# GpSimd instead of VectorE for the attention's low token halves, in a four-layer convolution and attention kernel

## The reference

```python
# layer 0: three gates over (channel, row, column) pairs, mixed by a softmax over their pooled means
z = concat([x.max(1), x.mean(1)]); b_k = x * sigmoid(bn(conv7x7(z)))
# layer 1: 3x3 convolution, 256 -> 256, with a weight mixed from circulant projections
# layer 2: x * sigmoid(relu(mean(dwt_ll(x)) @ W1.T) @ W2.T)
# layer 3: shifted windows of 8 x 8 tokens, 8 heads of 32
xw  = windows(roll(x, -4, -4))
q, k, v = split(xw @ w_qkv + b_qkv)
attn = softmax(q @ k.T * dh ** -0.5 + bias + mask)
out  = roll(unwindow((attn @ v) @ w_o + b_o), 4, 4)
```

## Time and profile before

| | |
|---|---|
| median of 3 runs | 2843.7 us (2843.35 to 2851.99) |
| the profiled execution | 2844.92 us, its span 2843.1 us |
| PE | 2312.9 us, 81% of the span |
| DVE | 2243.9 us, 79% |
| ACT | 1621.7 us, 57% |
| POOL | 1442.8 us, 51% |
| mean granted clock of PE | 0.941 |

### The profile page before, as it was taken

The page is one execution under the profiler, slowest core; times in us unless marked ns, Lnnn a source line. Parts: engine busy times, 40 slices in busy tenths (PEclk is TensorE's granted clock), DMA queues, the critical chain, the costliest instruction groups (busy, mean ns, idle before and its releaser), DMA issues. The chain is left out here.

```text
span 2843.1 us, 67589 instructions
## 1 busy us (share of the span) xinstructions
PE 2312.9 (81%) x27254; PEld 1321.7 (46%) x27254; DVE 2243.9 (79%) x3739; ACT 1621.7 (57%) x4072; POOL 1442.8 (51%) x1149
## 2 busy tenths in 40 slices
PE   0357738898888988898888978898889988899887
PEld 0233325455554545454554445454554445444454
DVE  7887956888888887888788887888888887886444
ACT  0322037754875567654876467754876567755554
POOL 2414552455735574456635474456635574455344
PEclk9868868999999999999999999999899999999989
DMA  5400400114110421114110411114110421111111
GB/s 150 123 3 15 168 3 17 31 67 142 31 40 25 141 66 32 31 68 142 32 46 24 142 61 32 31 68 142 32 46 24 142 61 32 31 60 46 46 46 39
DMA packets 125431, 176.20 MB, mean 62 GB/s; under 512 B 72496, under 2 KB 114240, under 8 KB 115520
## 3 DMA queue, kind: packets, MB, share of 16 engines
q1 hardware_dynamic: 125120, 171.88, 19.2%
HBM read 98.95 MB, written 72.86 MB: 60 GB/s over the span
## 5 line engine op out<-in xcount | busy, mean ns | idle before, releaser
L2048 PE MATMUL F<-g_raw,cw_hi 128*128 128x512 f16 x2304 | 701.0, 386 | 54.6 <-DVE X L1462 23.0
L1172 ACT ACTIVATE xs<-xs,mx 128x64 f32<-128x64 f32 x1792 | 445.8, 335 | 79.4 <-DVE mx L1813 79.4
L892 POOL TENSOR_TENSOR xs<-xs,rec 128x512 f32<-128x512 f32 x256 | 292.7, 1153 | 344.5 <-DVE rec L1823 343.5
L2048 PE MATMUL F<-g_raw,cw_lo 128*128 128x512 f16 x1152 | 444.0, 385 | 0.0
L2048 PEld LDWEIGHTS F<-g_raw,cw_hi 128*128 128x128 f16 x2304 | 222.0, 99 | 327.0 <-DVE X L1462 30.3
L1179 ACT ACTIVATE prt<-PTR 128x512 f32<-128x512 f32 x256 | 151.4, 591 | 259.2 <-PE PTR L2149 229.7
L877 POOL TENSOR_TENSOR tmp<-X,uw 128x512 f32<-128x512 f32 x128 | 164.4, 1299 | 253.8 <-DVE X L1658 236.2
L907 POOL TENSOR_TENSOR ot_lo<-ot,ot_hi 128x512 f16<-128x512 f32 x128 | 153.7, 1222 | 221.2 <-ACT ot_hi L1193 182.2
L1802 DVE TENSOR_TENSOR xs<-SP,bias 128x1024 f32<-128x1024 f32 (+2 forms) x192 | 160.2, 862 | 117.0 <-issue 67.2
L1391 DVE SCALAR_TENSOR_TENSOR g_raw<-l0c,gn,g_raw 128x512 f16<-128x512 f32 x192 | 183.2, 996 | 55.6 <-ACT g_raw L1031 40.0
L1821 DVE TENSOR_REDUCE sums<-xs 128x16 f32<-128x1024 f32 x128 | 154.9, 1210 | 79.8 <-ACT xs L1167 42.3
(11 more groups left out here) (326 smaller groups left out, 5725.3 us busy)
## 6 DMA issues: line engine op xcount, KB each, us to landing
scratch_x<-X SPq DMA_DIRECT2D x32, 1024.0 KB, 4.8
xs<-scratch_x SPq DMA_DIRECT2D x56, 508.0 KB, 3.4
out_x<-xs SPq DMA_DIRECT2D x56, 508.0 KB, 2.8
X<-in_x SPq DMA_DIRECT2D x25, 1024.0 KB, 6.4
l0c<-scratch_t SPq DMA_DIRECT2D x8, 1876.0 KB, 10.2
l0c<-in_x SPq DMA_DIRECT2D x7, 1024.0 KB, 5.0
l0c<-scratch_t SPq DMA_DIRECT2D x8, 640.0 KB, 12.2
l0c<-scratch_t SPq DMA_DIRECT2D x8, 576.0 KB, 13.5
```

Of the source, the lines that this page charges most:

```text
L892: G.tensor_tensor(keyed(sc[:, u % 4, :]), keyed(sc[:, u % 4, :]), rec[:, u % 4, :].unsqueeze(2).to_broadcast([P, 8, TOK]), ALU.mult).then_ ...
L1172: last = S.activation(keys, keys, ACT.Exp, bias=mx[:, u % 4, i:i + 1])
L2048: last = T.matmul(F[:, n % 2, :], wgt[:, ci, C3 * comp + dx, P * co:P * co + P], win[which], start=(ci == 0 and dx == 0 and j == 0), stop= ...
```

## The change

`low_tokens` and its stream `token_rows` move from VectorE's block to GpSimd's, with the same operands and the same semaphores; ScalarE's tokens and TensorE's fills wait for `tok_lo_set` as before. GpSimd's play gets the stream K, VectorE's loses it. The tables of all five engines are written anew. The number of pieces of each stream is the same, but for K; on GpSimd `AHEAD` of O goes from 2 to 1 and that of E from 1 to none, on ScalarE that of X from 1 to 2, on VectorE that of E from 2 to 1.

```diff
 TURN = {
...
-    "POOL": {"norm0a": "RRRRREO", "norm0b": "R", "reduce0": "RN", "reduce1": "NRNN", "reduce2": "R", "reduce3": "R",
...
+    "POOL": {"norm0a": "RRR", "norm0b": "N", "reduce0": "RKKR", "reduce1": "R", "reduce2": "RRN", "reduce3": "RN",
...
@@ GpSimd
+                def low_tokens(r, t):
+                    pool.wait_ge(tok_hi_set, CT * r + t + 1)
+                    if r:
+                        pool.wait_ge(qp_done, FILL[f"v1.{r - 1}"] + 1)
+                    G.tensor_tensor(tok_lo[:, t, :].rearrange("p (w i j) -> p w i j", w=NW, i=WS),
+                                    tok[:, t, :].rearrange("p (i w j) -> p w i j", w=NW, i=WS),
+                                    tok_hi[:, t, :].rearrange("p (w i j) -> p w i j", w=NW, i=WS),
+                                    ALU.subtract).then_inc(tok_lo_set, 1)
+
+                def token_rows():
+                    for r in range(ROWS_ALL):
+                        for t in range(CT):
+                            low_tokens(r, t)
+                            yield r
...
                 play("POOL", M=main(load, front), Y=setup(), R=sums(), D=lower_differences(), W=weighed_rows(), E=excitation(),
-                     X=centred(), N=normalised(), O=heads())
+                     X=centred(), N=normalised(), O=heads(), K=token_rows())
@@ VectorE
-                def low_tokens(r, t):
-                    dve.wait_ge(tok_hi_set, CT * r + t + 1)
-                    if r:
-                        dve.wait_ge(qp_done, FILL[f"v1.{r - 1}"] + 1)
-                    V.tensor_tensor(tok_lo[:, t, :].rearrange("p (w i j) -> p w i j", w=NW, i=WS),
...
                 play("DVE", M=main(load, front), Y=setup(), C=first_stats(), U=maxima(), B=lower_lifts(), J=joined_rows(),
-                     V=row_sums(), E=excitation(), K=token_rows(), S=score_units(), T=totals(), P=last_values(),
+                     V=row_sums(), E=excitation(), S=score_units(), T=totals(), P=last_values(),
                      A=additions())
```

More of the change, by code:

```diff
@@ L52 @@
 FIRST = {
[25 rows of a table removed]
[8 rows of a table added]
+        "convend": "RRRRERRRRRRRRR"},
[12 rows of a table added]
+        "convend": "JVJJVCVCVCUVVVVVEUUUECCCUECUEECEUCUUUEECUE"},
+    "PE": {"reduce11": "Y", "hwgate": "YY", "hwmean6": "YY", "gate11": "Y", "norm1c": "Y", "conv9.1": "Y",
+        "conv23.1": "EEE", "convend": "EEE"},
 }
 TURN = {
[35 rows of a table removed]
-        "convend": "JJJVVVVVVVVVECEECEESCESCE"},
[11 rows of a table removed]
-        "convend": "SQSEQE"},
[36 rows of a table added]
+        "convend": "JJJVVCVVVVVCVVECEEEESCECESCE"},
+    "PE": {"norm0c": "QQT", "reduce0": "Q", "reduce2": "Q", "reduce3": "TQ", "reduce4": "WTWQ", "reduce5": "S",
+        "reduce6": "WSQ", "reduce7": "TW", "reduce9": "Q", "reduce11": "Q", "reduce14": "Q", "reduce15": "QT",
+        "hwconv": "QWTQWTQ", "hwgate": "TWQ", "hwrows": "WSQS", "band1": "Q", "bandturn": "T", "hwmean0": "Q",
[9 rows of a table added]
 }
-AHEAD = {"SP": {"S": 1}, "POOL": {"R": 28, "E": 1, "N": 4, "O": 2}, "ACT": {"X": 1, "T": 4, "O": 1}, "DVE": {"U": 13, "E": 2, "A": 2, "T": 2}, "PE": {"Q": 2, "T": 4, "W": 4}}
+AHEAD = {"SP": {"S": 1}, "POOL": {"R": 28, "N": 4, "O": 1}, "ACT": {"X": 2, "T": 4, "O": 1}, "DVE": {"U": 13, "E": 1, "T": 2, "A": 2}, "PE": {"Q": 2, "T": 4, "W": 4}}
 LAST_ROWS = {
-    "SP": "SLSLSLSLSLSLSLSSLS",
-    "POOL": "EONNNXNXONXXNNXXNNXONXNNXXONXXNNXNXONXNXNNXXNOXXNNNXXOXXNNNNXXXONXNNNXXNXNXONNO",
-    "ACT": ("KKTKXTQKQQQTKKKTXOXQTQXXTQKQTXXKTOKKTQTXXQQTKQKKTOXXQQTXXQTQTXTXKKOKKQXTQQQXKTTKTKXXKOKXTXKQQTTQTQKX"
-            "OKXKQTQXXQQTTKXTXOKKXTXQTQQQKTXTXTOXTXTTOK"),
-    "DVE": "ETEAKKATSPSPKTKAATSTSPKPKAATSPKSTKAAPTSTPPKKASATSTSKPKPAATSPSKKATAPTSSTPKKAAPTSTSPPTATAASA",
-    "PE": ("QQTTQQQQQWSTQSWTWWQQQTQQTQQSTWQSWTWWTQQWQTQQQQTQSWTWWSQQQTQQQTQWSQTWTWSWQQQQTQQTQSWWTQTWSWTQQQQTQTWW"
-            "QTQSQSWWQQQQTQQTSWTWTSQWWQQQTQTQQQTWWSTQWQWSTTQWTWTWWQQQ"),
+    "SP": "SLSLSLSLSLSLSLSSSL",
+    "POOL": "KKNNNNXXOKKNXNXNNXXNOXKKXNNNXXOKXNKNXNNXKXONKXNXNNXKXOKNXNXNNXXOKKXNXNNNXXXONXKNKNNXXONXXNNNO",
+    "ACT": ("KKXXQQQTKQTTTXKOXKKTXQXQQKQTTKXTXOKKXKTXKQQTQQTTXOXKXKKTQXQQKTQKXTKTXOTXQXQKKQTQTTKOXXKXQTTXQKQQTKTO"
+            "KKXXQKQXTXTQQTTKXXOKXKXTQQTQQTTOXXTKXXTTKTO"),
+    "DVE": "EAATTSPPSTAATSTSPAAPTSSAPTPATSSPPTAATSPSTPAATSSPAPATTSSTAPTAPSPSTPTTAAASA",
+    "PE": ("QQQQQTQTQSTWWWTWSQQQQTQTQQWSWQTQTWSWTQQWQQTQQWSTTWSWQQQQTQTQQQQWTSWQSWTWQQTQQTQQQWTSTWQWWSQQQTQTQWWQ"
+            "TTSWWSQQQQQQTQWTQSTQWTSWWQQTQTQQQWQSTWTQWWSQTQQTWTTWWWQQ"),
 }
@@ L1781, in excitation @@
                         yield "coefs"
-                def low_tokens(r, t):
-                    dve.wait_ge(tok_hi_set, CT * r + t + 1)
-                    if r:
-                        dve.wait_ge(qp_done, FILL[f"v1.{r - 1}"] + 1)
-                    V.tensor_tensor(tok_lo[:, t, :].rearrange("p (w i j) -> p w i j", w=NW, i=WS),
-                                    tok[:, t, :].rearrange("p (i w j) -> p w i j", w=NW, i=WS),
-                                    tok_hi[:, t, :].rearrange("p (w i j) -> p w i j", w=NW, i=WS),
-                                    ALU.subtract).then_inc(tok_lo_set, 1)
                 def scores(u):
@@ L1841, in last_values @@
                             yield name
-                def token_rows():
-                    for r in range(ROWS_ALL):
-                        for t in range(CT):
-                            low_tokens(r, t)
-                            yield r
                 def score_units():
```

## The result

The change takes 2875.7 us (median of 4 runs, 2871.2 to 2878.1) against 2846.0 us for the kernel before, timed on the same chip. The ratio is 1.0096, with an interval of 1.0081 to 1.0111. I had forecast 2820 us with a chance of 0.57 for faster. The sign was wrong, and 2876 also lies above the range, which ended at 2870.

The account below looks back on a forecast made before the run. PE and VectorE were taken to share the limit, GpSimd having room. 4.7 - 1.0 - 0.3 gave 3.4 us an image, seven times 23.8; 2844.9 - 23.8 - 1.2 gave 2820 us. The range ran from 2778 to 2870.

Parts of the forecast that it names:

- What leaves VectorE: 128 low-half subtractions, 16.5 us an image; gain 3.7 us in the gate stage, 1.0 in the channel reductions, nothing elsewhere.
- the last rows give nothing: Last eight attention rows, 16 halves moved to GpSimd: put at 0, between a gain of 4.8 and a loss of 7.5 us.
- Contention: VectorE operations with two SBUF inputs slow beside a busier GpSimd: 1.0 us an image, bounds 0 and 7.3.
- Lateness: PE's q fill waits for a longer low half on GpSimd, once an image: 0.3 us.
- The rival of late halves: Halves queue on GpSimd behind the convolution's corrections, delaying q fills: 7.5 us lost against 3.7 won an image, 2870 us, chance 0.17.
- The orders: All engines' rewritten orders: put at 0; bounds plus and minus 37.7 us a stretch, 18 us in image 0's front.
- VectorE near 2120: Sign over the whole span: VectorE would be busy near 2120 us.
- GpSimd near 1600: Sign over the whole span: GpSimd would be busy near 1600 us.
- PE's waits for `tok_lo` under 3 us an image: Sign: PE would wait for GpSimd's low halves under 3 us an image.
- The stretches of 317 us: Sign: the seven repeated stretches, 320.5 us before, would come near 317 us.
- the counterparts of lines 1391 and 1623: Sign: these VectorE operations with both inputs from SBUF would get a few per cent longer.
- my signs of being wrong: Stretches staying at 320 with idler VectorE, q fills waiting 5 us or more an image, or change in first 384 or last 216 us.

Follow-up runs that it names:

- split_turn: As split, but with the low halves of the last eight rows of windows all back on VectorE: 2832.0 us, 0.9948 of the kernel before.
- split: Kernel before, old orders, with 8 of 16 low halves an image and 11 of the last 16 moved to GpSimd: 2827.4 us, ratio 0.9933.
- after_none: The change's new orders, with no low half made on any engine after the first row of windows: 2871.3 us, 1.0079 of the kernel before.
- move_only: Kernel before with its old orders on all engines, only the low halves moved from VectorE to GpSimd: 2851.6 us, ratio 1.0018.
- none_at_all: Kernel before, old orders, with no low half made on any engine after the first row of windows: 2820.0 us, ratio 0.9906.

## Why the prediction was wrong

Its sum was 4.7 - 1.0 - 0.3 an image and nothing for the orders. The step that failed is the last: the orders, put at nothing, cost 24 us with the moved work in them and 51 without. By steps:

- **What leaves VectorE, 4.7 us an image, 33 in all.** Right in kind, a little large. With no load anywhere the gain is 26 us, 3.4 of idle PE in an image. That most of the 16.5 us would be hidden was right. That the last rows give nothing was probably not: by split_turn they gave 4.7 us of split's 19, within what two overlapping intervals can show, and at the upper bound of 4.8 that I had named.
- **Contention, 1.0 us an image.** For the move it was about right: against before, VectorE's other work grew by 5.1 us over the span where I had 7. The 36 us seen in the change are not the moved operation's, since 35 of them are there in after_none, where it is left out.
- **Lateness, 0.3 us an image.** I asked only what the low half itself is late for. In the old orders this failed as well: PE's waits for the halves did double, from 10.8 to 24.7 us in move_only, and pieces behind them on GpSimd moved back too. In all, the load takes 32 us back there (2851.6 - 2820.0), some 4 an image. Five letters an image put elsewhere give half of it back, so at least that half is the delay of what stands behind. In the new orders the same load costs 4 us by the medians, where contention and lateness made 9 in my sum. For the change itself the term was not shown to be too small.
- **The rival of late halves.** It was to decide from 0.46 us a row on, and the load of 3.9 us of idle PE in an image is 0.49 a row: that is why the move alone ends near zero. The rival took 0.94, of which 0.58 was called half an `ot_lo`, and half of 1.22 is 0.61. Its reason, halves stuck behind the corrections, was tested by no run. That its 2870 us lies near the result is luck: in the change PE's waits for low halves are 3.3 us in all.
- **The orders, nothing.** This step failed whichever way the parts are taken. On top of the move they cost 24 us: 11 in the first image's part, where I had written 0 between plus and minus 18, and 13 in the rest. Without the moved work they cost 51. I had put the bounds of the repeated part at plus and minus 37.7 us an image and then taken the middle, because the number of pieces is unchanged. The middle of such bounds is a guess, and my range took almost nothing of their lower end.
- **The parts as measured** are -26 + 32 + 24 = +30 us by way of move_only, and -26 + 51 + 4 = +29 by way of after_none. Both sums must give the change's 29.6 us, since each part is the difference between two kernels on the way; they are no check of the account. What they show is that load and orders can't be priced apart. By the first way either of the two would have used up the relief or nearly so, and only both together make the kernel clearly slower; by the second the orders alone do it.

Of the signs that I named, VectorE near 2120 (2153), GpSimd near 1600 (1574) and PE's waits for `tok_lo` under 3 us an image (0.4) came true or nearly. The stretches of 317 us did not; they are what none_at_all and split show, 316.1 and 317.4. Nor did the counterparts of lines 1391 and 1623 grow by a few per cent: they grew by 14 and 25 (996 to 1139 ns, 1420 to 1774). And of my signs of being wrong one holds in part: 11 us of the orders' 24 sit in the first image.

## What to carry to other kernels

When work goes to an engine that is half idle, its price isn't only its own deadline but also that of whatever stands behind it there, and so it depends on the order (here 32 us in one and 4 in another): look through the engine's list for the links of a chain, and put the new work behind them, in a gap that the trace shows ahead of its use. Try the move with the old order first, and with a gap-fitted subset; here half of the operations brought three quarters of what was to be had. And an order written anew is a change of its own, to be timed without the work that it was written for.

## What the runs showed of the hardware

I had taken contention as a share of a mean. The trace shows it to be pair by pair. Before, 120 of the 192 coefficient operations of line 1391 run without a GpSimd operation ending beside them, none longer than 755 ns and at 748 on average. The other 72 average 1409 ns, and each ended 0.55 us behind the end of the GpSimd operation beside it. In the change 97 are of the first kind, at 749 ns, and 95 of the second, at 1537, of which 7 met only the last 0.16 us of a GpSimd operation and lost nothing; the other 88 again end 0.55 us behind. One pair of each, on the timeline (start us, us); before, VectorE and GpSimd:

```profile
1524.18 2.49 DVE L1391 SCALAR_TENSOR_TENSOR g_raw<-l0c,gn,g_raw 128x512 f16<-128x512 f32 x2 [0.86 <-ACT g_raw L1031]
```
```profile
1522.19 3.06 POOL L849 TENSOR_TENSOR l0c<-X 128x896 f32<-128x896 f32 x1
```

and the change:

```profile
1551.09 4.08 DVE L1406 SCALAR_TENSOR_TENSOR g_raw<-l0c,gn,g_raw 128x512 f16<-128x512 f32 x2 [0.86 <-ACT g_raw L1046]
```
```profile
1549.23 2.90 POOL L892 TENSOR_TENSOR xs<-xs,rec 128x512 f32<-128x512 f32 x2 [0.45 <-DVE rec L1829]
1552.09 2.53 POOL L849 TENSOR_TENSOR l0c<-X 128x896 f32<-128x896 f32 x1
```

The same two operations take 2.49 us beside the tail of one GpSimd subtraction, and 4.08 us where GpSimd's list has three in a row; the second of the two took 2.57 us of that. In both pairs the VectorE operation that had met line 849 ended 0.55 us behind the end of line 849 (1525.25 and 1554.62 us), wherever it had begun. It waited for the rest of that operation, however long that was. The Trainium skill (SBUF — State Buffer, Who interferes with whom) says that a VectorE instruction with two SBUF inputs contends with a GpSimd instruction that reads SBUF, and that the one that comes second is blocked for the whole instruction; the trace agrees for the case in which VectorE comes second, with these 0.55 us. What follows for a sum is that neither the number of operations nor their busy time sets the contention, but which of them the order puts side by side: 128 more GpSimd operations left the mean at 999 ns, while the new repeated order took it to 1150.
